# Value products of a tile in one stretch, and new step orders for two stages

## The reference

```
x = x + xcond0(layernorm(x), ctx)     # 16 heads of 32, 77 keys
x = x + ffn0(layernorm(x))            # 512 -> 64, a small per-channel network, 64 -> 512
x = x + xcond1(layernorm(x), ctx)
x = x + routed(layernorm(x))          # local windows of 64 (8 heads of 64) + a heavy path
```

## Time and profile before

| | us |
|---|---|
| median of 3 runs | 3358.11 (3357.79 to 3361.97) |
| the profiled execution | 3335.21 |
| its span, first to last instruction | 3333.4 |
| PE busy | 3165.0 (95%) |
| DVE busy | 2600.2 (78%) |
| POOL busy | 1614.3 (48%) |
| ACT busy | 1543.6 (46%) |

### The profile page before, as it was taken

How to read it: one execution, slowest core, us unless ns; L and a number is a source line. 1 busy time by engine, 2 the same in 40 slices (tenths; PEclk the granted TensorE clock), 3 DMA queues, 4 the chain that set the end, 5 groups by cost and what they waited for, 6 DMA issues and landing times.

```text
span 3333.4 us, 52524 instructions
## 1 busy us (share of the span) xinstructions
PE 3165.0 (95%) x20930; PEld 2429.6 (73%) x20930; DVE 2600.2 (78%) x4310; ACT 1543.6 (46%) x2509; POOL 1614.3 (48%) x1043
## 2 busy tenths in 40 slices
PE   6999999999999999999979999998999999987998
PEld 3677777777777777777757777776777777765886
DVE  3688888888889999999857888888888885656553
ACT  1466656566665555555533333332233333334443
POOL 0465655555566656666513444443345444465210
PEclk8999999999999999999989999998999999998999
DMA  4101010101112111111110111111122222132100
GB/s 150 34 28 51 26 53 26 53 26 58 55 47 72 50 37 50 50 51 36 64 70 27 57 51 51 51 51 51 33 86 92 70 76 76 40 117 70 36 20 13
DMA packets 87444, 180.04 MB, mean 54 GB/s; under 512 B 9526, under 2 KB 10294, under 8 KB 85664
## 3 DMA queue, kind: packets, MB, share of 16 engines
q1 hardware_dynamic: 82656, 161.99, 14.4%
q0 software_dynamic: 3968, 10.50, 1.1%
q10 hardware_dynamic: 576, 4.19, 0.3%
HBM read 106.05 MB, written 70.60 MB: 53 GB/s over the span
## 4 chain that ended last, share of the span: by engine, by line
PE 80%; DVE 13%; issue 3%; ACT 2%; POOL 1%; DMA 0%; SPq 0%; POOLq 0%; DVEq 0%; ACTq 0%
PE ps L255 15%; PE ps L257 14%; PE ps L256 14%; PE ps L250 11%; PE ps L262 7%; PE ps L451 6%; PE ps L461 4%; PE ps L1089 3%; PE ps L1069 2%; DVE rcol L1230 2%; PE ps L1662 2%; DVE dw L1191 1%; DVE sTa L546 1%; PE ps L1645 1%; DVE Sw L1180 1%
## 5 line engine op out<-in xcount | busy, mean ns | idle before, releaser
L793 POOL TENSOR_TENSOR Sb<-Sb,dn 128x1232 f32<-128x1232 f32 x128 | 288.5, 2254 | 298.3 <-DVE dn L591 298.3
L1477 POOL TENSOR_TENSOR Sw<-Sw,dw 128x2048 f32<-128x2048 f32 x64 | 231.3, 3614 | 383.6 <-DVE dw L1194 383.6
L733 ACT COPY PT<-ps 77x512 f32<-77x512 f32 x512 | 295.4, 577 | 157.4 <-PE ps L451 157.3
L250 PE MATMUL ps<-KB,QT 128*128 128x308 f32 x1024 | 342.4, 437 | 1.3 <-DVE XB L603 1.2
L1472 POOL TENSOR_TENSOR Sw<-Sw,mw 128x2048 f32<-128x2048 f32 x64 | 233.0, 3641 | 227.7 <-DVE mw L1186 227.7
L788 POOL TENSOR_TENSOR Sb<-Sb,mx 128x1232 f32<-128x1232 f32 x128 | 295.6, 2309 | 89.3 <-DVE mx L583 88.8
L451 PE MATMUL ps<-ident,Sb 128*77 128x128 f32 x2048 | 300.6, 277 | 2.5 <-ACT PT L733 1.3
L451 PEld LDWEIGHTS ps<-ident,Sb 128*77 128x77 f32 x2048 | 243.4, 148 | 68.6 <-issue 34.0
L1421 ACT COPY PU<-ps 128x512 f32<-128x512 f32 x256 | 137.9, 588 | 335.6 <-PE ps L262 335.5
L577 DVE TENSOR_TENSOR Sb<-ps,dlt 128x308 f32<-128x308 f32 x512 | 235.3, 460 | 62.5 <-PE ps L250 62.4
L262 PE MATMUL ps<-ident,xn 128*128 128x128 f32 x1120 | 173.5, 287 | 63.7 <-DVE xU L1153 29.5
(11 more groups left out here) (275 smaller groups left out, 8173.1 us busy)
## 6 DMA issues: line engine op xcount, KB each, us to landing
XB<-in_x SPq DMA_DIRECT2D x16, 1024.0 KB, 5.4
x_scratch<-XB SPq DMA_DIRECT2D x16, 1024.0 KB, 4.5
XB<-x_scratch SPq DMA_DIRECT2D x16, 1024.0 KB, 5.9
x_scratch<-XB SPq DMA_DIRECT2D x64, 256.0 KB, 2.0
XL<-x_scratch SPq DMA_DIRECT2D x64, 256.0 KB, 3.4
XY<-x_scratch SPq DMA_DIRECT2D x64, 256.0 KB, 3.2
y_scratch<-XY SPq DMA_DIRECT2D x64, 256.0 KB, 3.5
out<-yo SPq DMA_DIRECT2D x64, 256.0 KB, 2.0
```

What stands on the lines that cost most here:

```text
L250: m = PE.matmul(outp, l, r, start=(i == 0), stop=(i == len(pairs) - 1))
L733: A.copy(PT[:, 4 * g:4 * g + 4, :], ps[0:NK, bank("PT", n, g), :].rearrange("p (c n) -> p c n", c=4)).then_inc(a_pt, 1)
L793: G.tensor_tensor(sv, sv, last(dn[:, n % 2, :], NK), ALU.mult).then_inc(g_norm, 1)
L1477: G.tensor_tensor(sv, sv, last(dw[:, n % 2, :], 256), ALU.mult).then_inc(bg_norm, 1)
```

## The change

The two steps of a tile's value products become one step, at one place, in both stages. Inside it the products keep their sequence and their two semaphore increments; the wait for each copied piece stands ahead of the heads that read it. And every place in the tables of stages one and two is new (stage three's is not touched). The functions that use the places are the same.

```diff
-TILE = {"scores": (10, 15, 37, 39), "sadd": (7, 34, 44, 67), "smax": (92,), "sub": (-34,), "softexp": (132,),
-        "den": (150,), "norm": (55,), "ptrans": (235, 236, 278, 293), "pcopy": (216, 256, 282, 296), "pv": (312, 330),
-        "ohi": (313,), "olo": (337,), "wo": (385,), "xadd": (407,), "store": (485,)}
-LATE = {"xstat": (444,), "rsx": (306,), "zrow": (473,), "route": (523,), "comb": (659,)}
-PREP = {"stats": (-406,), "aggr": (-404,), "rstd": (-526,), "ln": (-342, -318, -275, -231),
-        "bias": (-263, -208, -172, 50), "turn": (-292, -236, -172, -171), "xhi": (-306, -235, -195, -191),
-        "low": (-289, -232, -186, -179), "q": (-121, -65, -36, -34), "qcopy": (-129, -50, -48, -30)}
+TILE = {"scores": (25, 32, 41, 48), "sadd": (16, 28, 37, 41), "smax": (80,), "sub": (-45,), "softexp": (137,),
+        "den": (152,), "norm": (48,), "ptrans": (238, 241, 272, 307), "pcopy": (228, 244, 283, 296), "pv": (335,),
+        "ohi": (321,), "olo": (332,), "wo": (382,), "xadd": (407,), "store": (681,)}
+LATE = {"xstat": (430,), "rsx": (345,), "zrow": (451,), "route": (496,), "comb": (814,)}
+PREP = {"stats": (-397,), "aggr": (-392,), "rstd": (-483,), "ln": (-354, -352, -257, -230),
+        "bias": (-76, -71, 167, 181), "turn": (-271, -235, -183, -174), "xhi": (-281, -253, -198, -196),
+        "low": (-279, -244, -181, -177), "q": (-123, -59, -41, -26), "qcopy": (-116, -48, -18, -13)}
...
-        "sT": (971,), "relu": (981, 997, 1021, 1043), "accu": (1006, 1012, 1042, 1045),
-        "wout": (1085, 1086, 1096, 1106), "fadd": (1050, 1053, 1083, 1091), "storeb": (1009,)}
+        "sT": (966,), "relu": (975, 994, 1034, 1040), "accu": (987, 1019, 1034, 1047),
+        "wout": (1085, 1092, 1111, 1112), "fadd": (1052, 1053, 1055, 1080), "storeb": (819,)}
...
-TILE_B = {"loadxy": (-63,), "scores": (-21, 4), "sadd": (5, 46), "smax": (56,), "sub": (76,), "softexp": (118,),
-        "den": (113,), "norm": (173,), "ptrans": (141, 142, 153, 159), "pcopy": (156, 157, 158, 164),
-        "pv": (169, 177), "ohi": (201,), "olo": (200,), "wo": (203,), "yadd": (246,), "yo": (412,), "storey": (186,)}
+TILE_B = {"loadxy": (18,), "scores": (-5, 20), "sadd": (5, 39), "smax": (56,), "sub": (136,), "softexp": (142,),
+        "den": (115,), "norm": (215,), "ptrans": (151, 156, 171, 174), "pcopy": (184, 186, 197, 205), "pv": (184,),
+        "ohi": (230,), "olo": (204,), "wo": (213,), "yadd": (229,), "yo": (477,), "storey": (270,)}
...
-GATHER = {"grows": (-248, -234, -213, -142, -88, -71), "gstats": (-19,), "grs": (38,), "gnorm": (18,),
-          "gsq": (52,), "gpow": (181,), "gfin": (148,)}
-ROUTE = {"rtp": 11, "rtv": 30, "rta": 35, "rts": -242}
+GATHER = {"grows": (-228, -148, -102, -44, -39, 91), "gstats": (82,), "grs": (216,), "gnorm": (127,),
+        "gsq": (505,), "gpow": (679,), "gfin": (1443,)}
+ROUTE = {"rtp": 25, "rtv": 37, "rta": 60, "rts": -102}
...
-            def pv(n, f):
-                p = bank("PV", n) if f else take("PV", n)
+            def pv(n, i):
+                p = take("PV", n)
                 pe.wait_ge(ld_VS[kvi(n) % 2], 16 * (kvi(n) // 2 + 1))
-                for g in (2 * f, 2 * f + 1):
-                    pe.wait_ge(a_pt, 4 * n + g + 1)
-                    for i in range(4):
-                        h = 4 * g + i
-                        m = PE.matmul(ps[32 * i:32 * i + 32, p, 128 * g:128 * g + 128],
-                                      VS[:, kvi(n) % 2, 32 * h:32 * h + 32], PT[:, h, :], start=True, stop=True)
-                m.then_inc(pe_pv, 1)
+                for h in range(16):
+                    pe.wait_ge(a_pt, 4 * n + h // 4 + 1)
+                    o = 32 * (h % 4)
+                    m = PE.matmul(ps[o:o + 32, p, 128 * (h // 4):128 * (h // 4) + 128],
+                                  VS[:, kvi(n) % 2, 32 * h:32 * h + 32], PT[:, h, :], start=True, stop=True)
+                    if h % 8 == 7:
+                        m.then_inc(pe_pv, 1)
```

More of the change, by code:

```diff
@@ L83, in nothing @@
     pass
-TILE = {"scores": (10, 15, 37, 39), "sadd": (7, 34, 44, 67), "smax": (92,), "sub": (-34,), "softexp": (132,),
-        "den": (150,), "norm": (55,), "ptrans": (235, 236, 278, 293), "pcopy": (216, 256, 282, 296), "pv": (312, 330),
-        "ohi": (313,), "olo": (337,), "wo": (385,), "xadd": (407,), "store": (485,)}
-LATE = {"xstat": (444,), "rsx": (306,), "zrow": (473,), "route": (523,), "comb": (659,)}
-PREP = {"stats": (-406,), "aggr": (-404,), "rstd": (-526,), "ln": (-342, -318, -275, -231),
-        "bias": (-263, -208, -172, 50), "turn": (-292, -236, -172, -171), "xhi": (-306, -235, -195, -191),
-        "low": (-289, -232, -186, -179), "q": (-121, -65, -36, -34), "qcopy": (-129, -50, -48, -30)}
-FEED = {"stats": (725,), "aggr": (747,), "rstd": (648,), "ln": (765, 766, 792, 807), "bias": (687, 769, 818, 858),
-        "turn": (767, 789, 794, 878), "xhi": (769, 803, 847, 862), "low": (794, 836, 845, 869), "win": (969,),
-        "sT": (971,), "relu": (981, 997, 1021, 1043), "accu": (1006, 1012, 1042, 1045),
-        "wout": (1085, 1086, 1096, 1106), "fadd": (1050, 1053, 1083, 1091), "storeb": (1009,)}
+TILE = {"scores": (25, 32, 41, 48), "sadd": (16, 28, 37, 41), "smax": (80,), "sub": (-45,), "softexp": (137,),
[5 more added lines that the diff above has]
+        "low": (-279, -244, -181, -177), "q": (-123, -59, -41, -26), "qcopy": (-116, -48, -18, -13)}
+FEED = {"stats": (720,), "aggr": (733,), "rstd": (585,), "ln": (767, 780, 796, 839), "bias": (832, 848, 850, 943),
+        "turn": (775, 796, 827, 885), "xhi": (784, 816, 820, 915), "low": (802, 845, 872, 919), "win": (970,),
+        "sT": (966,), "relu": (975, 994, 1034, 1040), "accu": (987, 1019, 1034, 1047),
+        "wout": (1085, 1092, 1111, 1112), "fadd": (1052, 1053, 1055, 1080), "storeb": (819,)}
 def order_a():
@@ L133, in walk_a @@
             do[name](*key)
-TILE_B = {"loadxy": (-63,), "scores": (-21, 4), "sadd": (5, 46), "smax": (56,), "sub": (76,), "softexp": (118,),
-        "den": (113,), "norm": (173,), "ptrans": (141, 142, 153, 159), "pcopy": (156, 157, 158, 164),
-        "pv": (169, 177), "ohi": (201,), "olo": (200,), "wo": (203,), "yadd": (246,), "yo": (412,), "storey": (186,)}
[L140 to L144, removed]
-GATHER = {"grows": (-248, -234, -213, -142, -88, -71), "gstats": (-19,), "grs": (38,), "gnorm": (18,),
-          "gsq": (52,), "gpow": (181,), "gfin": (148,)}
-ROUTE = {"rtp": 11, "rtv": 30, "rta": 35, "rts": -242}
+TILE_B = {"loadxy": (18,), "scores": (-5, 20), "sadd": (5, 39), "smax": (56,), "sub": (136,), "softexp": (142,),
+        "den": (115,), "norm": (215,), "ptrans": (151, 156, 171, 174), "pcopy": (184, 186, 197, 205), "pv": (184,),
+        "ohi": (230,), "olo": (204,), "wo": (213,), "yadd": (229,), "yo": (477,), "storey": (270,)}
+BLOCK_B = {"loadxl": (-766, -741, -690, -490), "tail": (-269,), "ln": (-650, -619, -561, -306),
+        "turn": (-319, -317, -299, -296), "xhi": (-294, -289, -266, -260), "xlo": (-298, -297, -294, -293),
+        "qk": (-278, -261, -258, -232, -202, -163, -143, -126),
+        "qkcopy": (-248, -217, -171, -162, -131, -111, -97, -72), "edge": (-53,), "v": (-96, -58, 1, 50, 59),
+        "vadd": (-32, -23, 26, 75, 78)}
+GATHER = {"grows": (-228, -148, -102, -44, -39, 91), "gstats": (82,), "grs": (216,), "gnorm": (127,),
+        "gsq": (505,), "gpow": (679,), "gfin": (1443,)}
+ROUTE = {"rtp": 25, "rtv": 37, "rta": 60, "rts": -102}
 def order_b():
@@ L1078, in ptrans, with pv @@
                 turn4(p, Sw[:, n % 2, 512 * q:512 * q + 512]).then_inc(b_pt, 1)
-            def pv(n, f):
+            def pv(n, i):
                 e = 17 * (n // 16) + n % 16
-                p = bank_b("PV", n) if f else take_b("PV", n)
-                pe.wait_ge(ba_pt, 4 * n + 2 * f + 2)
+                p = take_b("PV", n)
                 pe.wait_ge(bv_v, e + 2)
-                for c in (2 * f, 2 * f + 1):
+                for c in range(4):
+                    pe.wait_ge(ba_pt, 4 * n + c // 2 * 2 + 2)
                     for ck in (0, 1):
                         for r in (0, 1):
-                            pos = 4 * f + 2 * r + c % 2
+                            pos = 4 * (c // 2) + 2 * r + c % 2
                             m = PE.matmul(ps[64 * r:64 * r + 64, p, 128 * c:128 * c + 128],
@@ L1091, in pv @@
                                           PU[:, 2 * pos + ck, :], start=(ck == 0), stop=(ck == 1))
-                m.then_inc(b_pv, 1)
+                    if c % 2:
+                        m.then_inc(b_pv, 1)
             def wo(n, i):
```

## The result

The changed kernel took 3442.73 us (median of 4 runs, 3440.0 to 3449.58) where the kernel before took 3358.14 beside it: a ratio of 1.0254 [1.0241, 1.0267], +84.6 us. (Brackets behind a ratio are its 95% interval; every ratio is to the kernel before, run beside it.) It is slower, as forecast, but by more than twice the forecast 38 us, and above the range given, which ended at 3435.

What follows compares the result with a forecast made beforehand. TensorE was taken to bound stage one, with VectorE taking over in layer 1; stage two had unresolved waits. Layer 0 -26, layer 1 +77 and stage two -13 gave +38 us: 3396 us, range 3305 to 3435.

Steps and rivals of the forecast that it cites:

- Layer 1, the term said to decide: Layer 1: `route` moved directly behind `smax` makes VectorE the bound, +1.28 us a tile, +77 us over sixty tiles.
- the lock: Layer 1: GpSimd's `norm` and `sub` fully block VectorE's two-input line 621; loss 2.9 us a tile instead of 0.8.
- Rival (a): Layer 1: the lock is not met twice and TensorE stays the bound; -59 us, 3299 us; chance 0.27.
- Rival (b): Stage one: the fourth copied piece comes late in the merged value products; +21 us, 3417 us; chance 0.05.
- Rival (c): Layer 1: waits set by VectorE halve TensorE's clock; +51 us on top, 3447 us; chance 0.08.
- the one after "In layer 0": Layer 0: the query projection's 0.36 us wait goes in 14 blocks, 5 us; with the merge, -26 us together.
- a sentence that costed six moved steps: Stage one: moves of `ln`, `bias`, `rstd`, `storeb`, `store` and kv loads cost nothing, covered by engines with 35% to spare.
- Stage two was to give -13: Stage two: shorter waits for turned tiles, the end's `gsq` move and merged split pairs give -13 us; bounds 0 and -25.
- The turn's wait: Stage two: TensorE's 3.75 us wait falls to near 2.4 as `yadd` goes into blocked time; 8 us over six blocks.
- The sentence on index loads: Stage two: index loads stand later on SP but each still waits for the column before it, so they cost nothing.

Runs made afterwards that it cites:

- ring_bias_route_496: Changed kernel with `xstat` at 434, `comb` at 659 and bias additions one a tile ahead of `norm`, `route` kept at 496: ratio 1.0308 (1.0062 with `route` at 524).
- after_short_pool: Changed kernel with GpSimd's `sub` and `norm` of layer 1 working on 2 of 16 heads, all places unchanged: ratio 0.9939.
- after_route_524: Changed kernel with only `route` set back from 496 to 524, behind `xadd`, the first `sadd` and `low`: ratio 1.0177.
- after_ring_route496: Changed kernel with `xstat` at 434 and `comb` at 659, `route` left at 496: ratio 1.028.
- after_ring: Changed kernel with `route` at 524, `xstat` at 434 and `comb` at 659: ratio 1.0122.

## Why the prediction was off

Layer 1, the term said to decide, was right in mechanism and nearly in size. It had VectorE at 12.7 us a tile and line 621 at 2.1; the profile has 50.9 / 4 = 12.7 and 2.08. (The match is a little lucky: the lock adds 2 x (2.08 - 1.084) = 2.0 us a tile where 2.1 was forecast, and VectorE is busy for 12.2 of the 12.7 us, its waits for scores being 0.3 more.) Sixty tiles at +1.28 gave +77; the difference between the kernels grows by 86 from tile 64 to 127 (8.3 us at the start of tile 64's `norm`, 94.4 at 127's), of which 5.4 / 4 x 60 = 80 are the steady rate and the rest are the first tiles of the layer. One place carries it (1.29 us a tile by ring_bias_route_496), and that GpSimd is the holder is shown by after_short_pool. Rival (a), that the lock is not met twice, is refuted: the two are held in every tile, 1.08 or 1.67 us and 2.61, and VectorE is the bound. Rival (b) did not come: the stretch of 32 products takes 1.08 us, and TensorE waited in it for a copy only once in stage one, 0.7 us. Rival (c) did not come in the changed kernel: TensorE waited 34.6 + 13.8 us for 36 tiles, 1.3 us a tile in pieces of 1.5 at most, and the clock stayed at 1.00 in layer 1 (window above). In after_route_524, with waits of up to 3.9 us, it did fall, to a mean of 0.97.

The step that failed is the one after "In layer 0": "I let this 0.36 us go in 14 blocks, 5 us; the bounds are 0 and, if the accumulation comes late instead, a loss of the same 5. Layer 0 together: -26 us." Measured was about +7: the difference between the first profiles rises from 1.1 us at tile 4 to 8.3 at tile 64. The merge did its part (2.14 us for two scores groups and both halves, and 51.9 us for four tiles when nothing else waits, 1.7 less than before). Two waits took back 1.14 + 1.15 = 2.3 us a block, 34 over 15 blocks, which is the gap between -26 and +7. One is the accumulation, named in the prediction as a bound but priced at a third of its size: I had counted the chain on ScalarE (relu ahead of the copy) and not the step that now stands between the last two low halves on VectorE: it is two instructions, 2.30 us with the lock in it (GpSimd's L783 runs until 527.51; two such take 1.60 at 530.41, where GpSimd has no instruction). The other is `ln`, in a sentence that costed six moved steps "at nothing, covered by engines with 35% and more to spare". ScalarE has that much to spare, and the normalisation still came late, because it stood behind a copy that waits for TensorE: idle time is no cover for a step in a queue whose head waits.

The same sentence hid a second cause in layer 1, of some 3.7 us for four tiles once `route` is back at 524: 49.4 us, 48.0 with `xstat` and `comb` back as well, 45.75 with `bias` moved too. Of this 2.1 us is the lock again, on the two small instructions of `comb` under the bias additions. The rest is read from the waits as a ring (TensorE's projection waits for `olo`, 29.6 us in 400 in after_route_524; `xadd` waits for the projection, 30.7; `olo` stands behind `xadd`); that reading was not tested by itself. All this cost nothing in the changed kernel, as the lock on `route` was longer (after_ring_route496), so the sum was not hurt; but undoing `route` alone gives back only 611.1 - 592.8 = 18 of the 64 us (after_route_524).

Stage two was to give -13 and gave nothing (0.9999). The turn's wait fell from 3.75 to 3.15, not to 2.4. By size that is one `yadd` of 0.6 us out of the chain, not two; which one was not tried. Tiles 4 to 24 gained 6.9 us, more than these waits alone; what the rest is was not tried. The sentence on index loads ("so they cost nothing") looked at the wrong loads: `loadxy`, moved from -63 to 18, is now needed too soon after its issue for the one load that falls behind the weights, 5 us at the end of the stage (70.8 us for the last four tiles, 64.3 with the weights issued later).

As a sum, between the first two profiles up to the last tile of stage two: 1 at the start, 7 in layer 0 for -26, 86 in layer 1 for +77, -2 in stage two for -13, which is 92 for 38. (Between the second profiles the same is 88. Two profiles of the kernel before differ by 4.3 us, so 92 and the 85 of the medians are as near as this goes.) So layer 0 is 33 of the 54 that are missing. The misses of layer 0 and stage two have one form: what a moved step waits behind was not followed.

On the rule used for the lock: the Trainium skill's page "SBUF — State Buffer", section "Who interferes with whom", also says that a copy or a tensor_scalar may take the shared ports in a faster mode and then contend, and that the order of issue decides who blocks. The traces agree with both: the one-input L630 was held 1.2 us where it takes 0.17, the key copies 1.04 on average where they take 0.32 (both in after_ring), and `sub` itself 2.70 where it takes 2.25 when L621 was in first. Had I gone through VectorE's steps with it, `comb` and `kv` would have been on the list beside `route`; in the changed kernel they happen to miss GpSimd's work, in after_route_524 they do not.

## What to carry to other kernels

When two engines lock each other out, a step's place is a price: list for each GpSimd instruction which VectorE steps now fall under it, small ones too, since 0.17 us becomes 1.2. When a table of places is changed as a whole, a step's slack is not its engine's idle share but what the instruction at the head of its queue waits for; follow that for every moved step. For a load, ask how long before its use it is issued and what large load may stand ahead of it then. And a change that merges or removes work should be measured apart from the order it comes with: here the merge of stage one was worth 0.8% alone and 1.1% with two more places set for it (1.4% with the new stage two and its weights issued later), and the whole change -2.5% with the order that it came in.

## What was not expected of the hardware

The 16 us in stage three (215 to 218 us for 199 to 201) appear in some sets of runs and not in others, in the changed kernel (218 and 200 us in its two profiles) and in other orders of the same instructions; the trace shows VectorE and ScalarE waiting there for something that it does not name. A load of 256 KB issued behind 4 MB landed 15.6 us after its issue (13.2 in the kernel before), where the median of the 64 such loads is 3.4 us. Both are left as observed.
